# A state-space scan regrouped into steps of 4 states x 32 channels, 1024 columns wide, with its decays in SBUF

## What is computed

```python
def _L1_attn_ref(x, W_in, b_in, conv_w, conv_b, W_x, W_dt, b_dt, A_log, W_out, b_out):
    ...   # xc, res: two projections of x to 256 channels; u = silu(conv(xc))
    xp = u @ W_x.T
    dlt, Bm, Cm = jnp.split(xp, [dt_rank, dt_rank + n_state], axis=-1)
    delta = jax.nn.softplus(dlt @ W_dt.T + b_dt)
    A = -jnp.exp(A_log)                                  # 256 channels x 16 states
    dA = jnp.exp(jnp.einsum('bld,dn->bldn', delta, A))
    dBu = jnp.einsum('bld,bln,bld->bldn', delta, Bm, u)
    ...   # chunks of 32 tokens
    def step(carry, inp):
        a, bu, c = inp
        carry = a * carry + bu
        y = jnp.einsum('bkdn,bkn->bkd', carry, c)
        return (carry, y)
    ...
    y = y * jax.nn.silu(res)
    return y @ W_out.T + b_out
```

## Time and profile before

| | |
|---|---|
| median of 3 runs | 1052.18 us (1051.52 to 1057.14) |
| profiled execution | 1056.04 us |
| its span, first to last instruction | 1054.3 us |
| PE busy | 911.8 us (86%) |
| DVE busy | 768.3 us (73%) |
| ACT busy | 655.8 us (62%) |
| POOL busy | 516.0 us (49%) |
| mean granted TensorE clock | 0.937 of full speed |
| DMA | 151.83 MB, 144 GB/s over the span |

### The profile page before, as it was taken

The page is one execution under the profiler, slowest core; times in us unless marked ns, Lnnn a source line. Parts: engine busy times, 40 slices in busy tenths (PEclk is TensorE's granted clock), DMA queues, the critical chain, the costliest instruction groups (busy, mean ns, idle before and its releaser), DMA issues.

```text
span 1054.3 us, 11228 instructions
## 1 busy us (share of the span) xinstructions
PE 911.8 (86%) x3358; PEld 431.3 (41%) x3358; DVE 768.3 (73%) x1717; ACT 655.8 (62%) x1030; POOL 516.0 (49%) x412
## 2 busy tenths in 40 slices
PE   6557877888889888999999999999999889978975
PEld 5334334343444344445354444435443343333432
DVE  3222514988599769995999688978998989799821
ACT  4435558568757866677778765897687437634221
POOL 2112135555647464645565555666475545555311
PEclk9668898999899989999999999999999898998976
DMA  3000106523553446336337545545354717665320
GB/s 144 10 0 25 67 0 217 196 100 124 197 190 111 137 175 227 116 130 213 136 122 233 186 154 171 190 168 198 128 185 171 236 47 254 222 190 184 107 90 11
DMA packets 49325, 151.83 MB, mean 144 GB/s; under 512 B 4976, under 2 KB 13296, under 8 KB 49264
## 3 DMA queue, kind: packets, MB, share of 16 engines
q1 hardware_dynamic: 49264, 151.12, 41.9%
HBM read 148.21 MB, written 2.88 MB: 143 GB/s over the span
## 4 chain that ended last, share of the span: by engine, by line
PE 47%; DVE 26%; ACT 12%; issue 6%; POOL 5%; DMA 2%; SPq 0%; DVEq 0%; POOLq 0%; ACTq 0%
PE yp L1484 10%; DVE dA L983 10%; PE mp L1428 4%; PE mp L1443 4%; PE fp L1249 4%; PE pp L1363 4%; PE pp L1229 3%; PE fp L1265 3%; ACT L117 3%; DVE hs L990 3%; DVE he L941 2%; PE mp L1229 2%; PE pp L1333 2%; ACT dA L1208 2%; PE mp L1452 2%
## 5 line engine op out<-in xcount | busy, mean ns | idle before, releaser
L710 POOL TENSOR_TENSOR dbu<-du,b_row 128x1024 f32<-128x1024 f32 x128 | 301.5, 2359 | 169.7 <-DVE dA L983 151.0
L983 DVE TENSOR_TENSOR_SCAN dA<-dA,dbu 128x512 f32<-128x512 f32 x256 | 312.4, 1220 | 67.5 <-POOL dbu L710 34.9
L1484 PE MATMUL yp<-hs,ident 128*128 128x512 f32 x512 | 268.4, 628 | 14.1 <-DVE hs L990 13.9
L1208 ACT ACTIVATE dA<-delta,pr 128x512 f32<-128x512 f32 x256 | 173.6, 685 | 80.5 <-DVE hs L990 76.3
L990 DVE TENSOR_TENSOR hs<-dA,c_row 128x512 f32<-128x512 f32 x256 | 176.9, 691 | 9.8 <-PE yp L1484 1.1
L117 ACT ACT_TABLE_LOAD x130 | 166.8, 1283 | 2.4
L1484 PEld LDWEIGHTS yp<-hs,ident 128*128 128x128 f32 x512 | 89.2, 195 | 142.6 <-issue 84.8
L1428 PE MATMUL mp<-cont,ex_ 64*128 64x512 f32 x128 | 79.1, 701 | 12.7 <-DVE he L941 11.4
L1265 PE MATMUL fp<-w,hT 128*128 128x129 f32 x512 | 68.6, 285 | 13.7 <-ACT hT L1044 7.0
L1432 PE MATMUL mp<-cont,ex_ 64*128 64x512 f32 x128 | 79.3, 703 | 0.1
L1265 PEld LDWEIGHTS fp<-w,hT 128*128 128x128 f32 x512 | 64.2, 197 | 36.4 <-ACT hT L1044 14.9
(11 more groups left out here) (216 smaller groups left out, 1353.8 us busy)
## 6 DMA issues: line engine op xcount, KB each, us to landing
b_row<-held SPq DMA_DIRECT2D x104, 512.0 KB, 4.9
c_row<-held SPq DMA_DIRECT2D x104, 512.0 KB, 4.3
gsp<-gheld SPq DMA_DIRECT2D x64, 512.0 KB, 6.2
xin<-L_attn_x SPq DMA_DIRECT2D x8, 256.0 KB, 4.7
out<-xb SPq DMA_DIRECT2D x8, 256.0 KB, 3.4
ex_<-c_ex SPq DMA_DIRECT2D x1, 1001.0 KB, 6.8
b_row<-c_ps SPq DMA_DIRECT2D x1, 768.0 KB, 8.2
pr<-c_pr SPq DMA_DIRECT2D x1, 567.0 KB, 9.1
```

The costliest lines, as they stand in the source:

```text
L710: pool.tensor_tensor(out=dbu[:, j % 2, :].rearrange("p (r t) -> p r t", r=2), in0=d, in1=b_n, op=ALU.mult).then_inc(dbu_r.sem, 1)
L983: dve.tensor_tensor_scan(out=dA[:, half], data0=dA[:, half], data1=dbu[:, j % 2, half], initial=0.0, op0=ALU.mult, op1=ALU.add).then_inc(h ...
L1208: act.activation(out=dA[:, r * SEQ:(r + 1) * SEQ], in_=delta[:, i % 2, c, :], func=ACT.Exp, scale=mA[:, c, 2 * k + r:2 * k + r + 1]).then_ ...
L1484: pe.matmul(yp[:, :], lhsT=ident[:, :], rhs=hs[:, j % 2, r * SEQ:(r + 1) * SEQ], start=(s % PAIRS == 0 and r == 0), stop=(s % PAIRS == PAI ...
```

## The change

A step now covers two groups of 32 channels, and 4 states at a time. The partitions hold 4 blocks of 32 lanes: block s has the same 32 channels as the others, with 4 of the 16 states of its own. `delta` and `delta*u` are brought into that layout through DRAM: 128 channels x 512 are stored (L499, L504) and read back so that every 32-channel group stands on all four blocks (`u4`, `d4`; L509, L515). `B` and `C` come as 4 states on each block (`bc4`, L485), in two halves a batch, each with B and C of two of the four states. There are still 16 steps a batch, each 128x1024:

- ScalarE: two exponentials of 128x512 into `dA`, which is now in SBUF, two steps deep.
- GpSimd: `dbu`, 128x1024, from `u4` and `bc4`.
- VectorE: one scan of 128x1024, from `dA` and `dbu` into `hs`, all three in SBUF; one product of 128x1024 with `C`, in place in `hs`.
- TensorE: two matmuls of 512 columns with `stack`, four 32x32 identities one above the other, which add the four blocks into 32 partitions of `yp` for each channel group.

The two PSUM banks of `dA` become `qp`; its first half `mq` is the bank of the projections, which get a thread of their own (M, `S_TURNS`), and `pp` is left to the MoE fronts. `du` and `delta` have one buffer instead of two. `he` is gone: the experts' products are written over the gates in `gsp`, so that the four gate loads of a turn wait for the last expert matmul of the turn before (`eo_ps`). All five `ORDER` strings are new.

```diff
+BLOCKS = 4
+OWN = STATES // BLOCKS
+LANES = P // BLOCKS
+GROUPS = INNER // LANES
+PER = GROUPS // IC
+STEPS = IC * OWN * PER // 2
+STEP_ORDER = [(c, k, j) for c in range(IC) for k in range(OWN) for j in range(PER // 2)]
...
-        dA = pb("dA", [P, 2 * SEQ])
+        qp = pb("qp", [P, 2 * SEQ])
+        mq = qp[:, 0:SEQ]
...
-        delta = sb("delta", [P, 2, IC, SEQ])
-        du = sb("du", [P, 2, IC, SEQ])
+        delta = sb("delta", [P, IC, SEQ])
+        du = sb("du", [P, IC, SEQ])
+        dA = sb("dA", [P, 2, 2 * SEQ])
...
+                        sp.wait_ge(du_r.sem, du_r.at(i, c + 1))
...
+                        sp.dma_start(lanes(uheld), du[:, c, :]).then_inc(u_out[c].sem, 16)
...
+                        sp.wait_ge(u_out[c].sem, u_out[c].at(i, 16))
+                        if i >= 1:
+                            sp.wait_ge(dbu_r.sem, dbu_r.at(i - 1, (c + 1) * C_STEPS))
+                        sp.dma_start(u4[:, own, :].rearrange("p g t -> p (g t)"), groups(uheld)
+                                     ).then_inc(u_in[c].sem, 16)
...
-                            sp.wait_ge(her_e.sem, her_e.at(m - 1, part + 1))
-                            sp.wait_ge(her_o.sem, her_o.at(m - 1, part + 1))
+                            sp.wait_ge(eo_ps.sem, eo_ps.at(m - 1, 2))
...
+                        if n >= 2:
+                            pool.wait_ge(hs_r.sem, n - 1)
+                        b_n = bc4[:, k // 2, 0, k % 2, :].rearrange("p (a t) -> p a t", a=1)
+                        pool.tensor_tensor(out=dbu[:, n % 2, :].rearrange("p (r t) -> p r t", r=2),
+                                           in0=u4[:, c * PER + 2 * j:c * PER + 2 * j + 2, :],
+                                           in1=b_n.broadcast_to([P, 2, SEQ]), op=ALU.mult).then_inc(dbu_r.sem, 1)
...
+                        dve.tensor_tensor_scan(out=hs[:, n % 2, :], data0=dA[:, n % 2, :], data1=dbu[:, n % 2, :],
+                                               initial=0.0, op0=ALU.mult, op1=ALU.add).then_inc(hs_r.sem, 1)
...
+                        dve.tensor_tensor(out=two_h, in0=two_h, in1=c_n, op=ALU.mult).then_inc(hc_r.sem, 1)
...
+                            pe.matmul(yp[LANES * g:LANES * (g + 1), :], lhsT=stack[:, :],
+                                      rhs=hs[:, n % 2, r * SEQ:(r + 1) * SEQ], start=(k == 0), stop=(k == OWN - 1)
+                                      ).then_inc(sum_ps.sem, 1)
```

More of the change, by code:

```diff
@@ L118, in need, with last_of_half @@
             self.loaded = sets[0]
[L121 to L144, removed]
-    def loads_before(self, at, j_end):
-        return sum(self.slot[j] == at for j in self.after if j < j_end)
-B_ROWS, C_ROWS = Rows(B_SLOTS), Rows(C_SLOTS)
+BLOCKS = 4
[4 more added lines that the diff above has]
+STEPS = IC * OWN * PER // 2
+C_STEPS = STEPS // IC
+STEP_ORDER = [(c, k, j) for c in range(IC) for k in range(OWN) for j in range(PER // 2)]
+def last_of_half(h):
+    return max(s for s, (c, k, j) in enumerate(STEP_ORDER) if k // 2 == h) + 1
 PACKS = {
@@ L428, in build @@
         yg = sb("yg", [P, IC, SEQ])
-        b_in = [sem(f"b_in{k}") for k in range(B_SLOTS)]
-        c_in = [sem(f"c_in{k}") for k in range(C_SLOTS)]
-        dA_r = signal("dA_r", STEPS)
+        dA_r = signal("dA_r", 2 * STEPS)
         dbu_r = signal("dbu_r", STEPS)
@@ L643, in p_thread, with m_thread @@
                 half(b_enc).then_inc(ro_half, 1)
-                for kind, n in P_TURNS:
-                    if kind == "front":
-                        yield from front(n)
-                    elif kind == "mpre":
+                step(pool.memset(stack[:, :], 0.0))
+                for s in range(BLOCKS):
+                    ins = pool.affine_select(out=stack[:, :], in_=stack[:, :], compare_op=ALU.not_equal, fill=1.0,
+                                             base=-LANES * s, pattern=[[-1, LANES]], channel_multiplier=1)
+                    if s < BLOCKS - 1:
+                        step(ins)
+                ins.then_inc(consts, 1)
+                for m in range(len(M_TURNS)):
+                    yield from front(m)
+            def m_thread():
+                for kind, n in S_TURNS:
+                    if kind == "mpre":
                         if n == 0:
@@ L1402, in p_thread, with m_thread @@
                 pe.wait_ge(ro_ok, 2)
-                for turn_no, (kind, n) in enumerate(P_TURNS):
+                for m in range(len(M_TURNS)):
+                    yield from front(m)
+            def m_thread():
+                for turn_no, (kind, n) in enumerate(S_TURNS):
                     if kind == "mpre" and n == 0:
                         yield True
-                        bank_free(pe, turn_no)
+                        pe.wait_ge(w1_ok, 2)
+                        pe.wait_ge(w2_ok, 1)
                         pe.wait_ge(ld["ps"], 16)
-                        pe.matmul(pp[:, :], lhsT=cen[:, :], rhs=mw_in, start=True, stop=True).then_inc(pr_ps, 1)
+                        pe.matmul(mq, lhsT=cen[:, :], rhs=mw_in, start=True, stop=True).then_inc(pr_ps, 1)
                         yield True
```

371 lines of the change are left out of this document (189 added, 182 removed).

## The result

The changed kernel takes 1441.01 us (median of 4 runs, 1438.14 to 1443.18), the kernel before 1052.22 beside it: a ratio of 1.368, 95% interval [1.363, 1.373]. The forecast was 1178 us, with 1275 as its upper end. The direction was right, the size was not. The profiled execution took 1438.14 us, its span is 1436.4.

A forecast was written before the change was run, and what follows sets the result against it. VectorE's queue was taken to bound the kernel between first and last scan. Ahead 173 + 10, steps 445, places between them 436, waits 50, behind 66: 1180 us of span, median 1178 us, range 1075 to 1275 us.

The forecast's parts named there:

- the way through DRAM: Storing and reloading halves of `du` and `delta`: +10 us ahead of the first scan, later halves covered by the scan before.
- the stretch with scans: First scan's start to last scan's end, 815.5 us before; forecast as steps 445, places between them 436 and waits 50.
- the way through DRAM is late: Rival: SP holds `u4` loads behind a gate load waiting for TensorE, so halves start late; about 1260 us, chance 6%.
- Turn and turn: Likeliest case: VectorE and GpSimd operations on SBUF exclude each other, each waiting for the other; 1178 us, chance about 66%.
- case without exclusion: Rival: VectorE's scans and products run beside GpSimd without waiting; stretch 706 us, median 953 us, chance 13%.
- The waits: VectorE's remaining idle time between first and last scan: 50 us kept, with 0 to 115 possible.
- TensorE: Between first and last scan its busy time falls from 749 to about 615 us, and it ceases to be a bound.
- The sums into `yp`: TensorE's matmuls to different partition ranges run side by side, a step's two about 1.05 us instead of 2.1; 134 us saved.
- The steps alone: VectorE's 128 steps, each a scan of 2.28 us and a product of 1.20 us: 445 us, against 489 before.
- The gates: Gate loads after the last expert matmul: taken as nothing, since other work stands there anyway; uncovered 93 us.
- Behind the last scan: Chains of small dependent pieces after the last scan: 66 us, as in the kernel before (65.8).
- One-sided exclusion: Rival: VectorE waits for a running GpSimd operation, but GpSimd starts when it likes; 1083 us, chance 15%.

The follow-up runs named there:

- split run: Changed kernel with each 1 MB load of B and C, u or delta and each 256 KB store issued as four transfers of 32 partitions: 1217.2 us.
- the layout without the wide scan: Changed kernel with four transfers for each one, but decays in PSUM, 512-column scans, C product from PSUM, one bank, earlier order and more gate buffers: 1181.6 us.
- the control run: The kernel before, with only the order of its instructions changed on every engine: 1277.1 us, ratio 1.210.
- the PSUM operands: Changed kernel with the scan's decays and the C rows read from a constant in PSUM (decays and C left out of the result): 1348.5 us.
- both causes were gone: Changed kernel with loads and stores as four transfers each and decays and C from a PSUM constant (both left out of the result): 1039.8 us.

## Why the prediction was wrong, point by point

**The step that failed is the way through DRAM**, put as "+10 us" ahead of the first scan and as covered after it. Its price was read by bytes, from transfers of 4.7 and 6.8 us that have another outermost dimension than 4; the shape of the new ones stood in the diff. And the cover did not hold: ScalarE waited for `delta` once in every batch, 152.0 us in all. The split run gives the size: it takes back 27 us of the 46 by which the first scan was later than forecast, and 192 of the 207 by which the stretch with scans was longer (1138 against 931). With split transfers the stretch is 945.5 us, 14 from the forecast. The rival "the way through DRAM is late" (6%) named the place but not the cause (few DMA engines, not SP held by a gate load), and at 1260 us it was too cheap.

Not all of the 46 us are the way's. GpSimd's first `du` starts 11.4 us later than before (the first line is from the kernel before, the second from the changed one):

```profile
167.99 2.34 POOL L633 TENSOR_TENSOR du<-delta,du 128x1024 f32<-128x1024 f32 x1 [16.38 <-ACT delta L1152]
```

```profile
179.40 1.27 POOL L639 TENSOR_TENSOR du<-delta,du 128x512 f32<-128x512 f32 x1 [0.73 <-ACT delta L1170]
```

With one bank and the order of the kernel before, in the layout without the wide scan, it starts at 165.78. A new order alone put it at 179.41 in the kernel before (the control run). So the new order, perhaps with the bank of its own, is what makes it late, which is likely but not shown. From that start to the first scan it was 5 us before, and it is 50 in the changed kernel and 23 with split transfers. So the way adds 45 us there, and split still 18, not 10.

**Turn and turn** was the right mechanism, two-sided as forecast, and shown by the PSUM operands. On the side that the forecast had left open, GpSimd waiting for VectorE, the rule it cited from the Trainium skill ("SBUF — State Buffer", section "Who interferes with whom") agrees with the trace: 4.34 us for 2.36, 2.07 for 0.19. Its size was off: the forecast lies 225 us above its own case without exclusion, the runs show 177. The waits were too small by about as much: without exclusion the stretch was to take 706 us and took 766, of which VectorE was busy for 659, so that it idled for 107 us and not 50. The two errors hid each other in the sum, which is why 945.5 fits 931: that is luck. That other operations of GpSimd than `dbu` are held up as well, as its busy time going from 516 to 734 us shows, was not in it.

**TensorE** was to fall from 749 to 615 us of the stretch and took 725. Its share fell to 64% only because the stretch grew. The sums into `yp` took 147 us over the whole kernel, where 134 was forecast, and 132.7 where both causes were gone. But all other matmuls together went from 643 to 764 us of busy time (911.8 - 268.4 and 910.9 - 147.1), at a mean granted clock that fell from 0.937 to 0.78. With both causes gone the clock was 0.875 and TensorE's time in the stretch 648 us. How much of the 1441 us is due to the lower clock no run separates.

**The smaller terms.** The steps alone were right: the shortest scan takes 2256 ns, forecast 2.28 us, and the median product 1226, forecast 1205. The gates were taken as nothing, and as 93 us if uncovered; they cost 13 to 49 us, by what stands in the queue. Behind the last scan it is 69 us, forecast 66.

**The rivals.** No exclusion would have been 953 us; with exclusion and slow loads both removed the kernel took 1040, with 24 us more ahead of the first scan and 60 more in the stretch than that sum had. One-sided exclusion is refuted by the 4.34 us.

## What to carry to other kernels

Price a transfer by its shape, not by its bytes: look at what its outermost dimension is, and read the DMA share in a stretch where it is alone. Before an operand moves from PSUM to SBUF, ask what the other engine at SBUF does meanwhile; here the scan with its decays in SBUF cost 148 us once the transfers were split. Two causes at work together can hide each other: take away each alone and both together before giving either a price.

## What the runs showed of the hardware that was not expected

- Loads with an outermost dimension of 4 used 0.23 of the DMA engines (95 GB/s), pairs with an outermost 2 only 0.13 (52 GB/s), where the row loads before used 0.81 (256 GB/s). More transfers did not help; another outermost dimension did.
- A scan or product with two SBUF operands holds up small GpSimd operations as well as large ones: 0.19 us on four columns became up to 2.28 us. With one operand in PSUM the same operations never took over 0.198 us; the line is the group with the longest:

```profile
L573 POOL TENSOR_SCALAR f_vv<-f_mv x24: 192/193/198, 10.5 to 882.0; 128x4 f32<-128x4 f32 x24
```

- Four transfers of 32 partitions took SP 1.7 to 1.9 us to issue ahead of the first scan, where one took 0.5.
